# A gated MLP sandwich on one core: first x tile chunkwise, its gate and up products first, raw weights loaded in place of the low parts, and the early down products in another order

## The reference

```python
def attn(x, w_gate, w_up, w_down):
    s = silu(x @ w_gate.T)                       # 2048 x 1376
    # per token: the 688 entries of smallest |s| are set to 0
    s = s * (x @ w_up.T)
    return s @ w_down.T
x = x + layernorm(attn(layernorm(x), w_gate, w_up, w_down))
x = x + layernorm((silu(x' @ W_gate.T) * (x' @ W_up.T)) @ W_down.T)   # x' = layernorm(x)
```

## Time and profile before

| what | value |
|---|---|
| median of three runs | 719.76 us |
| profiled execution, its own time | 720.74 us |
| its span, first to last instruction | 718.9 us |
| PE busy | 706.9 us, 98% |
| DVE, ACT, POOL busy | 81%, 53%, 35% |

### The profile page before, as it was taken

One profiled execution on the slowest core, in us unless ns is written; L12 is line 12 of the kernel. 1 busy time (PEld: TensorE's weight loads), 2 busy tenths in 40 slices (PEclk: granted clock), 3 DMA queues, 4 the chain that ended last, 5 costly groups with the idle time before them and its releaser, 6 DMA issues.

```text
span 718.9 us, 9847 instructions
## 1 busy us (share of the span) xinstructions
PE 706.9 (98%) x3181; PEld 594.8 (83%) x3181; DVE 582.4 (81%) x1013; ACT 383.1 (53%) x610; POOL 248.4 (35%) x377
## 2 busy tenths in 40 slices
PE   8999999999999999999999999999999999999997
PEld 7888878888888888888888887877887888877885
DVE  6789778888898888987789889998688988877443
ACT  5896577677677566776654335433354333323230
POOL 1423123332323323233232666613315665621001
PEclk9999999999999999999999999999999999999999
DMA  8641424223554435544332677244953533334341
GB/s 276 200 110 63 100 70 98 56 78 87 124 130 83 100 86 116 128 84 111 102 107 72 174 232 217 87 156 115 247 143 111 161 119 111 93 111 147 137 142 44
DMA packets 126214, 88.56 MB, mean 123 GB/s; under 512 B 66416, under 2 KB 106608, under 8 KB 126160
## 3 DMA queue, kind: packets, MB, share of 16 engines
q1 hardware_dynamic: 126160, 87.91, 45.0%
HBM read 49.87 MB, written 18.87 MB: 96 GB/s over the span
## 4 chain that ended last, share of the span: by engine, by line
PE 68%; DVE 11%; issue 8%; ACT 5%; POOL 4%; DMA 3%; SPq 1%; DVEq 0%; ACTq 0%; POOLq 0%
PE gu_ps L813 14%; PE y_ps L754 13%; PE gu_ps L740 11%; PE tr_ps L813 10%; PE tr_ps L740 8%; PE gu_ps L835 4%; PE tr_ps L835 3%; ACT junk L937 3%; POOL move L1795 2%; PE gu_ps L788 2%; PE tr_ps L788 2%; PE y_ps L835 1%; DVE below L1376 1%; POOL thr L1798 1%; DVE xstat L1247 1%
## 5 line engine op out<-in xcount | busy, mean ns | idle before, releaser
L937 ACT ACTIVATE junk<-absv,thr 128x1383 bf16<-128x1383 f32 x96 | 139.1, 1449 | 43.4 <-POOL thr L1798 42.5
L754 PE MATMUL y_ps<-down_hi,hT 128*128 128x512 f32 x352 | 109.1, 391 | 0.0
L1795 POOL TENSOR_SCALAR move<-sgn 128x1 f32<-128x1 f32 x80 | 41.8, 522 | 108.0 <-ACT junk L937 108.0
L754 PEld LDWEIGHTS y_ps<-down_hi,hT 128*128 128x128 f32 x352 | 66.1, 188 | 14.4
L754 PE MATMUL y_ps<-down_lo,hT 128*128 128x512 f32 x176 | 69.5, 395 | 2.2 <-DVE hT L1279 2.2
L740 PE MATMUL gu_ps<-gate_hi,xT 128*128 128x460 f32 (+1 forms) x232 | 67.7, 373 | 0.0
L740 PE MATMUL gu_ps<-up_hi,xT 128*128 128x460 f32 (+1 forms) x232 | 67.2, 371 | 0.0
L1777 POOL TENSOR_TENSOR yrstd<-yvar,half 128x1 f32<-128x1 f32 x32 | 23.5, 736 | 85.3 <-DVE yvar L1288 85.3
L1770 POOL TENSOR_TENSOR xrstd<-xvar,half 128x1 f32<-128x1 f32 x32 | 21.9, 685 | 77.1 <-DVE xvar L1251 77.1
L1818 POOL TENSOR_TENSOR prod<-prod,gate_lo_raw 128x512 f32<-128x512 f32 (+1 forms) x20 | 26.1, 1305 | 64.3 <-DVE prod L1509 64.3
L740 PEld LDWEIGHTS gu_ps<-gate_hi,xT 128*128 128x128 f32 x232 | 44.1, 190 | 5.0
(11 more groups left out here) (306 smaller groups left out, 1923.2 us busy)
## 6 DMA issues: line engine op xcount, KB each, us to landing
absv<-prod SPq DMA_DIRECT2D x64, 176.0 KB, 3.4
h_scratch<-prod SPq DMA_DIRECT2D x38, 256.0 KB, 2.8
xin<-x_scratch SPq DMA_DIRECT2D x18, 256.0 KB, 2.7
xres<-in_L_attn_x SPq DMA_DIRECT2D x16, 256.0 KB, 3.4
x_scratch<-xres SPq DMA_DIRECT2D x16, 256.0 KB, 2.5
xg_even<-xin SPq DMA_DIRECT2D x64, 64.0 KB, 2.6
up_lo<-h_scratch SPq DMA_DIRECT2D x8, 512.0 KB, 3.8
up_hi<-h_scratch SPq DMA_DIRECT2D x8, 512.0 KB, 4.4
```

The costliest lines, as they stand in the source:

```text
L754: last = nc.tensor.matmul(y_ps[:, :], h, w[:, c, :], start=(c == 0 and i == 0), stop=(c == JC - 1 and i == 2))
L937: nc.scalar.activation(junk[:, 0:I + PAD], absv[:, q, A0 - PAD:A0 + I], ACT.Sign, bias=thr[:, q:q + 1], scale=-1.0, accum_out=sgn[:, q:q + ...
L1795: stepped(nc.gpsimd.tensor_scalar(move[:, :], sgn[:, q:q + 1], sgn[:, q:q + 1], float((WINDOW - 1) ** 2) + 0.5, ALU.mult, ALU.is_gt))
```

## The change

- The raw weight pieces are loaded straight to where their low parts will stand (`raw_w`), and the low part is written over the raw one. `stage` has no slots any more for them, no `load_w` waits, and each piece has a semaphore of its own. The waits between the first loads are gone.
- The first x tile is normalised, transposed and split in four chunks of 128 columns, each chunk in a PSUM bank of its own. PE's padding is 18 and 4 transpositions instead of 15 and 10.
- `first_product` makes tile 0's gate and up products: it starts with the eight matmuls that take the high weights and ends with the four that take the low ones.
- PE makes tile 0's gate and up first, then tile 1's gate, then its up. The transpositions of x tiles 1 and 2 move with it.
- down(j - 2) comes after the up third `max((9 - j) // 2, 0)`: for tiles 5, 6 and 7 one third later than before, for the others where it was.
- ACT and DVE: new orders through tile 3. Among them: abs_values(0) stands behind all twelve low parts of gate and up pieces; the three times_up of tile 1 stand before find_flag(0); split_h_hi(0) stands before count(1, 4), split_h_hi(1) before count(2, 4), split_h_hi(2) before count(3, 4); split_h_lo(2) stands before find_below(3) (`SOON`); y_stats(0) and x_normalise(4) stand behind swap_h(1). POOL's y_rstd(0) and its newton steps are ordered to match.
- Last stage: the copies of the last h are made for half 1 first, then half 0; two tile_lo stand before an x_normalise; the last tile's y_stats and add_residual of the first pass stand before two, respectively one, of the right_lo.

```diff
-    USEQ = [(0, 0), (1, 0), (0, 1), (0, 2), (1, 1), (1, 2)] + [(j, n) for j in range(2, TILES) for n in range(3)]
+    SOON = range(4, 5)
+    USEQ = GSEQ
...
+        def raw_w(w):
+            m, n, c = PIECES[w]
+            if m == 2:
+                return down_lo_raw[:, n:n + c, :]
+            raw = (gate_lo_raw, up_lo_raw)[m][:, :].rearrange("p (c i) -> p c i", c=KC)
+            return raw[:, c:c + 2, CO[n]:CO[n] + CW[n]]
...
             def load_w(w):
                 m, n, c = PIECES[w]
-                slot = w % NSLOT
-                if w >= NSLOT:
-                    sp.wait_ge(wlo_done, w - NSLOT + 1)
...
+                sp.dma_start(raw_w(w), src).then_inc(piece_in[w], 16)
...
             load_x(0)
             load_w(0)
             load_w(1)
-            sp.wait_ge(x_in[0], 16)
-            load_w(2)
-            sp.wait_ge(stage_in[0], 16)
-            load_w(3)
-            sp.wait_ge(stage_in[1], 16)
             load_x(1)
-            for w in range(4, 8):
+            for w in range(2, 8):
                 load_w(w)
...
+            def transpose_first_x():
+                for c in range(KC):
+                    if c < KC - 1:
+                        pe.wait_ge(xn_part, c + 1)
+                    else:
+                        pe.wait_ge(xn_done, 1)
+                    nc.tensor.transpose(first_x_bank(c), xin[:, 0, c * P:(c + 1) * P],
+                                        ident[:, :]).then_inc(x_tr_part if c < KC - 1 else x_tr, 1)
+
+            def first_product(m, n):
+                what = ("GU"[m], 0, n)
+                bank_free(what)
+                dst = bank(what)
+                for c in range(KC):
...
+                    if c % 2 == 0:
+                        pe.wait_ge(whi_done, 6 * m + 2 * n + c // 2 + 1)
+                    at = c * I + CO[n]
+                    for s in (1, 0):
+                        nc.tensor.matmul(dst[:, 0:CW[n]], xT[:, 0, s, c * P:(c + 1) * P], gu_hi[m][:, at:at + CW[n]],
+                                         start=(c == 0 and s == 1), stop=False)
+                for c in range(KC):
+                    if c % 2 == 0:
+                        pe.wait_ge(wlo_done, 6 * m + 2 * n + c // 2 + 1)
+                    at = c * I + CO[n]
+                    last = nc.tensor.matmul(dst[:, 0:CW[n]], xT[:, 0, 0, c * P:(c + 1) * P], gu_lo[m][:, at:at + CW[n]],
+                                            start=False, stop=(c == KC - 1))
+                last.then_inc((g_done, u_done)[m], 1)
...
-            keep_busy(15)
-            transpose_x(0)
-            keep_busy(10)
-            for n in range(2):
-                product(0, 0, n)
+            keep_busy(18)
+            transpose_first_x()
+            keep_busy(4)
+            for n in range(3):
+                first_product(0, n)
+            first_product(1, 0)
+            first_product(1, 1)
             transpose_x(1)
-            product(0, 0, 2)
+            first_product(1, 2)
...
-                    if n == max(6 - j, 0) and j < TILES - 1:
+                    if n == max((9 - j) // 2, 0) and j < TILES - 1:
                         down(j - 2)
...
+            split_x_hi(3)
+            split_weights_hi(17)
+            split_h_hi(0)
             count(1, 4)
             silu(2, 0)
-            split_h_hi(0)
-            split_weights_hi(17)
             count(1, 5)
...
                 normalise_y(j - 2)
+                if j + 1 in SOON:
+                    split_h_hi(j - 1)
                 count(j, 4)
...
+            last_h_hi(0, 1)
             last_h_hi(0, 0)
-            last_h_hi(0, 1)
             tile_hi(1, 0)
...
-            x_normalise(4)
-            swap_h(1)
-            for n in range(3):
-                times_up(2, n)
-            y_stats(0)
+            swap_h(1)
+            y_stats(0)
+            x_stats(4)
+            times_up(2, 1)
+            x_normalise(4)
             add_residual(0)
+            times_up(2, 2)
...
+                if j in SOON:
+                    split_h_lo(j - 2)
                 find_below(j - 1)
-                if 3 < j < LATE:
+                if 3 < j < LATE and j not in SOON:
                     split_h_lo(j - 2)
...
-                y_stats(TILES + r)
+                if r < S_TILES - 1:
+                    y_stats(TILES + r)
...
+                if r == S_TILES - 2:
+                    y_stats(TILES + r + 1)
                 for i in R_AT.get(r, ()):
+                    if i == TSEQ[-1]:
+                        add_residual(TILES + r)
                     right_lo(1, i)
```

More of the change, by code:

```diff
@@ L168, in sandwich @@
         down_lo = sb("down_lo", [P, JC, H], F32R)
-        with nc.sbuf_tensor("stage", [P, NSLOT, 2, H], F32) as stage:
+        with nc.sbuf_tensor("stage", [P, KC * 2 * GW], F32) as stage_flat:
             pass
@@ L348, in res_buf @@
             return xin[:, b % 2, :] if in_xin(b) else xres[:, b % 2, :]
-        stage_in = [sem(f"stage_in{i}") for i in range(NSLOT)]
+        piece_in = [sem(f"piece_in{w}") for w in range(NP)]
         pair_in = [sem(f"pair_in{i}") for i in range(NPAIR)]
@@ L386, in sandwich @@
         block = ctx.enter_context(nc.Block())
-        ring = [("G", 0, 0), ("G", 0, 1), ("G", 0, 2), ("G", 1, 0), ("G", 1, 1), ("G", 1, 2)]
-        ring += [("U", j, n) for j, n in USEQ[:6]]
-        for j in range(2, TILES):
+        ring = []
+        for j in range(TILES):
             ring += [("G", j, n) for n in range(3)] + [("U", j, n) for n in range(3)]
@@ L435, in x_bank, with first_x_bank @@
             return (tr_ps[1], tr_ps[2], tr_ps[1])[a]
+        def first_x_bank(c):
+            return (tr_ps[1], tr_ps[0], gu_ps[3], gu_ps[2])[c][:, 0:P]
         def x_place(a):
@@ L592, in _ @@
             move_h(0)
-            load_w(NP - 1)
             load_res(0)
@@ L962, in split_x_hi, with split_first_x_hi @@
                 nc.scalar.activation(hi, src, ACT.Copy).then_inc(xhi_done, 1)
+            def split_first_x_hi():
+                hi, _ = x_place(0)
+                for c in range(KC):
+                    if c < KC - 1:
+                        act.wait_ge(x_tr_part, c + 1)
+                    else:
+                        act.wait_ge(x_tr, 1)
+                    nc.scalar.activation(hi[:, c, :], first_x_bank(c),
+                                         ACT.Copy).then_inc(xhi_part if c < KC - 1 else xhi_done, 1)
             def split_h_hi(j):
@@ L1107, in _ @@
             guess(2)
-            for n in range(4):
+            for n in range(3):
                 count(2, n)
+            count(2, 3)
             normalise_y(0)
+            split_h_hi(1)
             count(2, 4)
-            split_h_hi(1)
+            split_x_hi(4)
             for j in range(3, TILES - 1):
-                if 3 < j < LATE:
+                if 3 < j < LATE and j not in SOON:
                     split_h_hi(j - 2)
@@ L1260, in x_normalise, with first_x_normalise, split_first_x_lo @@
                     nc.vector.transpose(xin[:, p % 2, :], xin[:, p % 2, :]).then_inc(xswap_done, 1)
+            def first_x_normalise():
+                dve.wait_ge(xr_done, 1)
+                for c in range(KC):
+                    at = xin[:, 0, c * P:(c + 1) * P]
+                    nc.vector.tensor_scalar(at, at, xmv[:, 0:1], xrstd[:, :], ALU.subtract,
+                                            ALU.mult).then_inc(xn_part if c < KC - 1 else xn_done, 1)
+            def split_first_x_lo(c):
+                if c < KC - 1:
+                    dve.wait_ge(xhi_part, c + 1)
+                else:
+                    dve.wait_ge(xhi_done, 1)
+                hi, lo = x_place(0)
+                nc.vector.tensor_tensor(lo[:, c, :], first_x_bank(c), hi[:, c, :].bitcast(F32),
+                                        ALU.subtract).then_inc(xlo_part if c < KC - 1 else xlo_done, 1)
             def swap_h(j):
@@ L1575, in _ @@
             split_weights_lo(13)
-            times_up(1, 2)
             split_weights_lo(14)
@@ L1580, in _ @@
             split_weights_lo(16)
+            split_weights_lo(17)
+            split_h_lo(0)
             find_below(1)
-            split_h_lo(0)
-            split_weights_lo(17)
             find_top(1)
             abs_values(2)
-            x_stats(4)
+            times_up(2, 0)
             find_flag(1)
             select(1)
+            swap_h(1)
+            y_stats(0)
+            x_stats(4)
+            times_up(2, 1)
             x_normalise(4)
-            swap_h(1)
-            for n in range(3):
-                times_up(2, n)
-            y_stats(0)
             add_residual(0)
+            times_up(2, 2)
             split_h_lo(1)
@@ L1687, in _ @@
                     tile_lo(0, 1)
+                if u in XU:
+                    x_normalise(XU[u])
                 gate1(u)
@@ L1822, in _ @@
             units(0)
+            newton(0, 0)
             x_rstd(2)
-            newton(0, 0)
+            newton(0, 1)
             x_rstd(3)
-            for n in range(1, STEPS):
```

(11 more changed lines are left out.)

119 lines of the change are left out of this document (52 added, 67 removed).

## The result

The changed kernel takes 722.05 us (median; 720.78 to 722.62), the kernel before 719.83 us on the same chip (719.01 to 720.96). The ratio is 1.0028 with a 95% interval of 1.0020 to 1.0036: slower, by more than the 0.2% that can be told. The predicted 718.0 and its range, up to 720.6, both miss. Run again beside later experiments (c2), the changed kernel took 721.8 against 720.29, ratio 1.0022 (1.0012 to 1.0031). One execution of all those timed, the eighth of e10, took 1179.95 us at a granted clock of 0.56; it is in no ratio, and without it e10's median is 718.87 and not 719.00.

The account below looks back on a forecast made before the run. PE was taken as the bound (busy 706.9 of 718.9 us), so only its waits could be won. Early gain 1.1 or -0.2 plus late 1.25 gave -2.35 or -1.05, middle -1.7: 719.76 becomes 718.0, range 715.0 to 720.6.

Parts of the forecast that it names:

- the chain: Selection from abs_values through counts, find, select, swap_h and DMAs to h's low part; PE's three waits, together 2.7 us, hang on it.
- The front: Start through tile 0's products: first product at 7.45 instead of 8.96, 1.5 us sooner, then fed by DVE.
- the earlier of my two times: Start of the first count in tile 0: 24.05 us if TensorE's clock rises early, against 25.3.
- the DMA rival: Front: at 276 GB/s weight pieces land late and all selections come 5 us later, 723.7 us; chance 0.11.
- the case of the early clock: First product: clock at 2.4 GHz by 7.4 us, product (0,0) ends at 10.1; total change -2.35 us; even chances.
- the upper case: Later set of times, for a clock rising at 10.6: h(0) at 56.6, down(4) at 146.9, total change -1.05 us.
- the late clock: First product: clock rises again at 10.6 us, product ends at 11.5, x_lo(1) 1.25 us later; even chances.
- Tile 1: Selection from h(0)'s landing to h(1)'s: 21.3 us, h(1) at 76.6 or 77.9 against 77.05 before.
- The no-change rival: Early part gives back 1 us more through one more POOL move beside DVE work in tile 1: 719.5 us; chance 0.15.
- Tiles 2 to 4: down(2) gains 1.6 us, h(3) lands 1.7 later; early gain 1.1 or -0.2 us through down(6).
- The late parts: Last stage: 0.55 us at the end of pass one, 0.7 in its last rows; gain 1.25 us.
- the slower rival: DMA sets the front's pace: 723.7 us at 276 GB/s, about 722 at 300; chance 0.11.

Follow-up runs that it names:

- e10: Kernel before with down products of tiles 3 to 5 one up third later and tile 8's x parts made sooner: 719.00 us, ratio 0.9973.
- e5: Changed kernel with count(1,4) and silu(2,0) in front of split_h_hi(0) on ACT: 722.32 us, ratio 1.0031 to the kernel before.
- e3: Kernel before with only the down products of tiles 3 to 5 one up third later: 719.62 us, ratio 0.9998.
- e12: Kernel before with all edits of the last stage and nothing else: 719.99 us, ratio 0.9996.
- e9: Changed kernel, tile 1's low parts spread, count(1,4) before h(0)'s copies, tile 8's x sooner, h(2)'s early copies undone: 719.34 us, ratio 0.9978.

## Why the prediction was wrong

Right was the frame: PE sets the time where the chain lets it, and what the front wins on PE is worth nothing. The steps, one by one:

**The front.** The first product came at 6.97 (7.45 forecast), and the clock had risen by then, the case that I tied to the earlier of my two times. The chain still went by the later one or worse: first count 25.80 (24.05 or 25.3). The step took 385 GB/s and let pieces land 1.2 us apart from 7.3 on. The queue reached that rate only from 8 us on (307 GB/s from 4 to 6), ACT took piece 2 as it landed at 9.22, and it still waited for transfers at 17.27 and 20.82, where 18.8 was forecast for the last. This is the DMA rival in small: at most 1.75 us against the case of the early clock, not five. That the upper case then fits the rows up to down(4) is luck in part: it stood for the late clock, and late transfers filled its place.

**Tile 1.** h(0) landed at 56.66 (56.6 forecast), h(1) at 78.49 (77.9); c2 has 56.33 and 77.98. The no-change rival was "one more POOL move beside DVE work (1.2)"; e5 shows 4.65 us for move and sum. The landing hid them from the time, and also hid that they were there, so they are not why h(1) is late in the changed kernel. The price of down(1)'s late landing is its stall of 1.64, which takes back PE's lead.

**Tiles 2 to 4.** h(3) lands 23.60 after h(2) (23.85 forecast), down(3) and down(4) wait 0.84 and 0.43, and down(4) starts at 147.15 (145.6 or 146.9; 146.87 for the old order). So at down(4) the upper case of the forecast held within 0.3 us, with h(1) and h(2) 0.6 and 0.5 late.

**The step that failed** is the next: "At down(6), in its old place again, the chain's slack of 2.3 ... is used up and takes 0.2 more". I followed the chain to down(6) and looked only at h's low part. In tile 7 the order of both queues changes: x tile 8's copy stands behind count(7,2) and its low part behind swap_h(6). This queue had about 0.9 us of slack before (low part done at 178.75, asked for at 179.62), and the chain came 2.59 later (h(5) lands at 165.90, not 163.31). So it cost 1.56, and down(6) started 1.92 later and not 0.2. e2, which moves only these parts, takes the stall away; e3 and e10 show the same wait and its cure on the kernel before. The stall takes both, this place and the late chain: e1 leaves the parts where they were and only undoes the early copies of h(2), and it is gone there too.

**The late parts** were given 1.25 us; e12 measures 0.3 (at most 0.9). The two waits I counted away were real, but the one at 555 differs from 0 to 1.16 between executions of the same code, and the gain at the end of pass one is lost again in part where down_tile(0) waits. With the edits the loads for pass two's first left parts also take 0.6 to 1.6 us longer to land, and this stops PE in some executions. I named the last right_lo as late by half a microsecond and did not ask what the transfers behind it meet.

Together: the upper case, -1.05, plus 1.7 up to down(6) (1.92 late instead of 0.2, of which 1.56 is tile 8's x), plus 0.95 for the late parts (0.3 won instead of 1.25), is +1.6. The two pairs of profiles show 1.2 and 1.1, the timed runs 2.2 (interval 1.4 to 2.6) and 1.5 (0.9 to 2.2), so the sum lies within both. Behind down(6) the two pairs win 0.7 and 0.8, more than e12 measures; how much of this is the random landing of transfers stays open.

The measured 722.05 is also where the slower rival had its case of 300 GB/s, and its sign came, ACT waiting on a transfer until 17.27. That is luck: e1 and e2, which change nothing in the transfers, each take more than half of the loss away.

Not separated is the front's chunkwise start from the orders of tiles 0 and 1: no kernel had one without the other. That e10 with the old front is no slower than e9 with the new one and the late edits says only that together they are worth nothing.

## What to carry to other kernels

When a chain of work is allowed to come later, walk down each engine's queue behind it until the order repeats, and ask of every instruction who needs it next: the slack at the product that you look at need not be the smallest. A wait that hides another wait leaves no row; a small instruction that takes six to nine times its usual time (1.73 for 0.29, 2.91 for 0.34) beside a busy neighbour is the row that tells of it. And a wait seen in one profile is worth its size only if a second profile of the same kernel has it too.

## What the runs showed of the hardware

POOL's one-column sum took 2.91 us at 53.34 in the changed kernel and 0.34 at 60.16; its move 1.73 and 0.29. The rows of DVE beside the long ones are subtractions with both operands in SBUF, 50.84 to 56.8. In the same kernel the move at 48.12 took 1.28 beside select(0), which reads two operands in SBUF, and the sum at 49.50 only 0.34 beside swap_h(0), which reads one. The Trainium skill (SBUF — State Buffer, SBUF: two separate sides) says that DVE and GpSimd share a pair of ports as an exclusive lock, which an operation of DVE with two SBUF inputs holds for the whole instruction against a GpSimd operation that reads SBUF. The trace agrees, and adds that GpSimd did not get in where one DVE instruction followed the next: one subtraction of a whole piece takes 1.1 us, and the sum began at 53.34, while two of them ran one behind the other from 53.85 to 56.20, and ended at 56.25.

TensorE's clock rose from 1.2 to 2.4 GHz, by the pitch of its instructions (transpositions start 0.213 us apart before and 0.11 after), in the first product, between 9.4 and 10.9 us, in four of the eight profiles with the old front and 15 padding transpositions, and before 6.1 in the other four, with the same code there. In nine of the ten with 18 it rose before the first product, between 4.3 and 7.6, in e9 with its first matmul, at about 7.5. In e12 it rose inside the padding, before any product or any x transposition (15 in 3.17 us, against 3.46 in the earlier trace rows):

```profile
1.66 3.17 PE L851 MATMUL y_ps<-ident 128*128 128x128 f32 x15 [1.66 <-DVE prod L1226]
```

So here transpositions alone (128x128 in float32) brought the clock up, against the sentence of the Trainium skill that the prediction cites for the later rise; before the rise the engine had made nothing but padding. The clock decided little: with the old front and 15 transpositions h(0)'s copies began at 54.9 to 55.8 in the profiles with an early rise and at 55.5 to 55.8 in those with a late one.
